# Reordering maxima waves, value products and statistics in the pixel attention of a fused four-block kernel

## The reference, cut to what matters

```
xn  = group_norm(x2, gn_scale, gn_bias)              # 32 groups of 8 channels
q, k, v = split(w_qkv @ xn + b_qkv)                  # 8 heads of 32 channels
w   = softmax(q^T k / sqrt(32), over the 1024 keys)  # 1024 x 1024 per image and head
h   = w @ v
out = x2 + w_proj @ h + b_proj
```

## Time and profile before

| what | value |
|---|---|
| median of the runs | 1919.95 us |
| profiled execution, span | 1922.28, 1920.5 us |
| TensorE busy | 1666.5 us, 87% |
| VectorE busy | 1376.5 us, 72% |
| ScalarE busy | 790.9 us, 41% |
| GpSimd busy | 1360.7 us, 71% |
| chain that ended last | PE 57%, DVE 30%, issue 5%, ACT 3%, POOL 2%, DMA 2% |
| its largest lines | DVE MX L1327 18%, PE AV L684 8%, PE RB L932 6% |
| TensorE waits for L1327 before the weight load of L632 into S | 84.4 us, 195 times |
| one reduction of 128 x 512 to maxima | 681 ns |
| load of an input tile pair (1024 KB), issue to landing | 4.9 us; in the windows shown issued at 859.96 |

### The profile page before, as it was taken

How to read it: one execution, slowest core, us unless ns; L and a number is a source line. 1 busy time by engine, 2 the same in 40 slices (tenths; PEclk the granted TensorE clock), 3 DMA queues, 4 the chain that set the end, 5 groups by cost and what they waited for, 6 DMA issues and landing times.

```text
span 1920.5 us, 37066 instructions
## 1 busy us (share of the span) xinstructions
PE 1666.5 (87%) x15160; PEld 768.6 (40%) x15160; DVE 1376.5 (72%) x2121; ACT 790.9 (41%) x1546; POOL 1360.7 (71%) x581
## 2 busy tenths in 40 slices
PE   6898656799999999999999999999997689889974
PEld 2333223344344444444444444444442355555541
DVE  5767577887777777777777777777771157878875
ACT  0443410255445455454454455454555233333320
POOL 0584500298888878878878878788689068988996
PEclk8898877799999999999999999999998889999986
DMA  5000030300001001010010010010010201222211
GB/s 189 1 2 1 1 129 0 146 15 24 2 23 45 2 24 45 2 46 23 1 60 9 2 67 2 1 67 2 2 46 1 89 29 52 84 82 75 74 51 47
DMA packets 48431, 75.10 MB, mean 39 GB/s; under 512 B 30804, under 2 KB 31110, under 8 KB 48262
## 3 DMA queue, kind: packets, MB, share of 16 engines
q1 hardware_dynamic: 38758, 72.15, 10.5%
q10 hardware_dynamic: 9504, 0.59, 0.3%
HBM read 44.87 MB, written 25.17 MB: 36 GB/s over the span
## 4 chain that ended last, share of the span: by engine, by line
PE 57%; DVE 30%; issue 5%; ACT 3%; POOL 2%; DMA 2%; SPq 0%; POOLq 0%; DVEq 0%; ACTq 0%
DVE MX L1327 18%; PE AV L684 8%; PE RB L932 6%; PE AV L945 3%; PE S L632 3%; PE S L720 3%; PE RB L720 3%; PE RB L981 3%; DVE HI L1304 2%; DVE LO L1305 2%; PE RB L710 2%; PE RB L738 2%; PE RB L745 1%; PE S L606 1%; PE S L960 1%
## 5 line engine op out<-in xcount | busy, mean ns | idle before, releaser
L1238 POOL TENSOR_TENSOR ACC<-ACC,PR 128x1024 f32<-128x1024 f32 x360 | 843.7, 2386 | 25.6 <-ACT PR L1075 25.3
L1075 ACT ACTIVATE PR<-S 128x512 f32<-128x512 f32 x687 | 388.7, 603 | 383.8 <-PE S L670 258.2
L1327 DVE TENSOR_REDUCE MX<-S 128x1 f32<-128x512 f32 x660 | 431.5, 681 | 103.7 <-PE S L632 56.0
L1238 POOL TENSOR_TENSOR ACC<-PR 128x1024 f32<-128x1024 f32 x72 | 169.6, 2379 | 351.7 <-PE S L699 156.3
L684 PE MATMUL AV<-PR,VT 128*32 128x512 f32 x2304 | 306.1, 609 | 2.3 <-ACT PR L1075 2.3
L632 PE MATMUL S<-HI 32*128 32x512 f32 x660 | 259.6, 483 | 17.5 <-DVE MX L1327 11.3
L1075 ACT ACTIVATE PR<-RB 128x512 f32<-128x512 f32 x316 | 187.8, 603 | 101.8 <-PE S L670 42.0
L1327 DVE TENSOR_REDUCE MX<-RB 128x1 f32<-128x512 f32 x300 | 201.3, 680 | 22.3 <-PE RB L632 13.9
L655 PE MATMUL S<-HI 32*128 32x512 f32 x687 | 194.7, 467 | 2.8 <-DVE X L1520 2.3
L632 PEld LDWEIGHTS S<-HI 32*128 32x128 f32 x660 | 106.1, 188 | 189.5 <-DVE MX L1327 84.4
L1264 POOL TENSOR_TENSOR PR<-WO,WRK 128x1792 f32<-128x1792 f32 x32 | 155.4, 4877 | 29.6 <-DMA WO<-WO 17.4
(11 more groups left out here) (352 smaller groups left out, 3477.4 us busy)
## 6 DMA issues: line engine op xcount, KB each, us to landing
X<-out_y SPq DMA_DIRECT2D x24, 1024.0 KB, 4.9
out_y<-X SPq DMA_DIRECT2D x16, 1024.0 KB, 4.7
X<-in_x SPq DMA_DIRECT2D x8, 1024.0 KB, 8.5
OHU<-out_y SPq DMA_DIRECT2D x8, 512.0 KB, 4.0
X<-out_y SPq DMA_DIRECT2D x8, 512.0 KB, 4.0
out_y<-X SPq DMA_DIRECT2D x8, 512.0 KB, 3.1
out_y<-OHU SPq DMA_DIRECT2D x8, 512.0 KB, 3.2
WO<-WO SPq DMA_DIRECT2D x128, 16.0 KB, 1.8
```

The source lines that it names most:

```text
L1075: nc.scalar.activation(exps(s, pair)[:, HALF * one:HALF * one + HALF], RING[ring.place()], ACT.Exp, scale=1.0 if i is None else float(D) * ...
L1238: nc.gpsimd.tensor_tensor(ACC[:, pair, :], so_far, exps(s, pair), ALU.add).then_inc(pool_used, 1)
L1327: nc.vector.tensor_reduce(out=MX[:, h, t, keys:keys + 1], in_=bank(), op=ALU.max, axis=AX.X).then_inc(ring_free, 1)
```

## The change

`values` becomes a job of the list. A half's first step has now both waves in front of its other jobs. A middle step is as before. A half's last step has the max wave, the values of the step before, the late wave, `negate`, its other jobs, its own values, and `flip`. The statistics of a second window (`ahead` = 2) go from steps 11 and 13 to 9 and 12, and the first `gn` from 15 to 13. The ring is filled in the new order. Computation and data stay the same.

```diff
--- before.py
+++ after.py
@@ -110,7 +110,7 @@
 
     if job[0] == "v":
         return 2 if single else 1
-    return {"max": 2, "late": 2, "stats": 0, "negate": 0, "reread": 0, "concepts": 4, "softmax": 0, "turn": 4,
+    return {"max": 2, "late": 2, "stats": 0, "negate": 0, "values": 0, "reread": 0, "concepts": 4, "softmax": 0, "turn": 4,
             "classes": 2, "norms": 2, "pool": 0, "regate": 0, "write": 4}.get(job[0], 1)
 
 
@@ -135,16 +135,8 @@
 
 
     jobs = [[] for _ in range(STEPS)]
-    late = [[] for _ in range(STEPS)]
     for half in range(2):
         first = MT * half
-        if half == 0 or nxt:
-            waves = maxima(1 - half)
-            for step in range(first, first + MT):
-                jobs[step].append(waves.pop(0))
-                late[step] = [("late",) + waves.pop(0)[1:]]
-            jobs[step] += late[step] + [("negate", 1 - half)]
-            late[step] = [("flip", 1 - half)]
         if half == 1 or trail:
             jobs[first + SUM_AT].append(("sums",))
             jobs[first + SPREAD_AT].append(("spread", half - 1))
@@ -157,15 +149,28 @@
         for step, job in zip((3, 5, MT + 4, MT + 7), ((0, 0), (1, 0), (0, 1), (1, 1))):
             jobs[step].append(("post",) + job)
     if ahead:
-        first = MT + 3 if ahead == 2 else MT
+        first = MT + 1 if ahead == 2 else MT
         jobs[first].append(("stats", 0, ahead))
-        jobs[first + (2 if ahead == 2 else 1)].append(("stats", 1, ahead))
+        jobs[first + (3 if ahead == 2 else 1)].append(("stats", 1, ahead))
         jobs[first + (4 if ahead == 2 else 3)].append(("gn", 0, ahead))
     if gn:
         jobs[MT + 5].append(("gn", 1, 1))
     for step, stage in side:
         jobs[step].append(stage)
-    return [job + waves for job, waves in zip(jobs, late)]
+    for half in range(2):
+        waves = maxima(1 - half) if half == 0 or nxt else []
+        for at in range(MT):
+            first, second, rest = waves[:1], [("late",) + wave[1:] for wave in waves[1:2]], jobs[MT * half + at]
+            waves = waves[2:]
+            ends = [("negate", 1 - half)] if first else [], [("flip", 1 - half)] if first else []
+            if at == 0:
+                rest = first + second + rest
+            elif at < MT - 1:
+                rest = first + rest + [("values", 0)] + second
+            else:
+                rest = first + [("values", 0)] + second + ends[0] + rest + [("values", 1)] + ends[1]
+            jobs[MT * half + at] = rest
+    return jobs
 
 
 
@@ -748,15 +753,9 @@
                 for s in range(STEPS):
                     ring.begin(jobs[s], i is None)
                     scores(u, par, s)
-                    last = s % MT == MT - 1
-                    behind = [job for job in jobs[s] if job[0] == ("flip" if last else "late")]
-                    for job in jobs[s][:len(jobs[s]) - len(behind)] + [("values",)] + behind:
+                    for job in jobs[s]:
                         if job[0] == "values":
-
-                            if s % MT:
-                                values(u, par, s - 1)
-                            if last:
-                                values(u, par, s)
+                            values(u, par, s - 1 + job[1])
                         elif job[0] == "spread":
                             spread(2 * u + job[1])
                         elif job[0] == "sums":
@@ -1404,6 +1403,8 @@
                             normalise(1 - par if job[1] else par, 1 if job[1] else 0)
                         elif job[0] == "sums":
                             ring.skip(1)
+                        elif job[0] == "values":
+                            pass
                         elif job[0] == "max" or job[0] == "late":
                             row_max(*job[1:])
                         elif job[0] == "negate":
```

## The result

The changed kernel takes 1934.81 us, the median of five runs (1929.35 to 1939.72), beside 1919.95 (1919.33 to 1923.85) for the kernel before: ratio 1.0077, 95% interval 1.0052 to 1.0102. The forecast was 1920.4 in 1911 to 1930. The profiled execution took 1939.45 (span 1937.7), 17.2 more than that of before, where the medians differ by 14.9.

What follows compares the result with a forecast made beforehand. Neither TensorE nor VectorE alone was the bound; whichever is late sets each step. Terms +6.1 - 1.8 + 0.6 - 1.0 - 1.6 - 0.9 - 0.9 = +0.5 gave 1920.4 us, range 1911 to 1930.

Steps and rivals of the forecast that it cites:

- (a): Last steps of a half, values between the waves: +0.32 in 19 steps (+6.1); with a residual -0.25 each (-1.8).
- (b): First steps with V, both waves in front: 3.50 grows to 4.46, step with sums falls from 5.00 to 4.08; +0.6.
- (c): Second windows, statistics and group sums earlier: steps 12 and 13 +0.91, step 14 -1.37, step 15 +0.23; -1.6 over seven.
- R1: Rival, slower: the step with sums doesn't return the stall in front of V; half of it about 10, 1930; chance 0.12.
- R3: Rival, faster: last steps follow TensorE, 4.6 instead of 5.13, 26 times: -13, 1907; chance 0.08.
- R4: Rival, faster: the moved statistics cost nothing, taken up by VectorE's slack: -11, 1909; chance 0.08.
- R2: Rival, slower: granted clock, one 1.2 GHz stretch in each of 7 windows, +10 less 3: 1927; chance 0.06.
- (d): Once each: batch 0's first window waits 0.9 less for statistics; a values step moved in the layer ahead gives -0.9.

Runs made afterwards that it cites:

- e9: Changed kernel plus one idle VectorE memset of 1024 columns ahead of L2's windows: 1930.84 us, ratio 1.0068 to the kernel before.
- e10: Changed kernel plus one idle VectorE memset of 2048 columns ahead of L2's windows: 1933.33 us, ratio 1.0069 to the kernel before.
- e7: Changed kernel without VectorE's second part of the statistics in second windows, that computation left out: 1912.24 us, ratio 0.9969 to the kernel before.
- e11: Against e8: the changed kernel's orders of waves, values and V everywhere, statistics still in pieces: 1913.54 us, ratio 0.9966 to the kernel before.
- e5: Changed kernel with the old order in the two windows of the layer ahead (L0): 1929.29 us, ratio 1.0047 to the kernel before.
- e8: Kernel before, values between waves only in last steps with a residual, second windows' statistics moved, second part in three pieces: 1899.08 us, ratio 0.9896.
- e4: Changed kernel with the statistics back in steps 11 and 13 and group sums in 15: 1938.95 us, ratio 1.0099 to the kernel before.
- e1: Kernel before with only the second windows' statistics moved to steps 9 and 12, first group sums to 13: 1916.45 us, ratio 0.9989.
- e2: Kernel before with only the values of the step before put between the two waves of last steps: 1933.59 us, ratio 1.0075.
- e3: Kernel before with only both waves put in front of V in a half's first steps that have V: 1923.49 us, ratio 1.0020.
- e6: e4 plus an unused matmul before the flip's wait in L2's windows behind batch 0's first: 1938.71 us, ratio 1.0101 to the kernel before.

## Why the prediction was wrong

**The sum of the steps was right.** (a), (b) and (c) came out within 0.05 per step, as the table shows, but for the 0.08 in step 10: VectorE's hole ahead of the late wave, ScalarE's 0.44 in front of V, the stall returned by the step with sums at 4.07 (R1's condition, over 4.28, was not met), and the statistics' wait turning up in step 13 as late drains. R3 and R4 fall by the same rows: last steps took 5.11 and not 4.6, step 13 took 4.88.

**The step that failed is R2, left out of the sum and held for 0.06.** The prediction put the clock into a rival and its argument against it was "five windows with nearly the same waits hold 1.00". That took undisturbed windows as proof that such waits are harmless. The traces show that a wait can be followed by a slow stretch or not with all steps the same (batches 2 and 5 beside 1, 3, 4 and 6 of the changed kernel; e9, e10), and that the changed kernel has other waits: in an undisturbed second window 1.5 in step 13 and 0.4 to 0.5 before the transposes and before V, where the one of before has 1.0 in step 12 and 1.1 in step 14; in a first window 0.4 to 0.5 before the transpose and before V, where before had none over 0.3. That the kernel before had one stretch in the thirteen windows from batch 1 on said little about the next order. The prediction's own sign of being wrong, a granted clock under 1.00 in windows that had none, is what came: 0.98 and 0.95 in batch 3.

**Its price was too low as well.** R2 counted one stretch per second window at 1.4, from the one window of before that had one; 1927 in all. After, one of 3.4 costs 1.6 (step 0, 6.08 instead of 4.44) and one of 6.8 costs 2.3 to 2.5 (steps 13 and 14, 11.39 instead of 8.92). Five stretches more, and four of the six twice as long as the one of before, are 11.4 of the +12.1 between the starts of batch 1 and of the last window.

**Term (d) failed by the clock too.** The -0.9 of the layer ahead became +3.1; in e7, e9 and e11, whose stretches lie otherwise there, it is -0.7 to -1.0, as forecast. Batch 0's first window, by the prediction's terms some 0.2 shorter (-0.9 for the statistics, twice +0.32), grew by 1.8: its steps 0 and 1 by 2.0, since its first V ran at 1.2 GHz (a stretch from 368.9 to 375.8), the others together by -0.2. The kernel before has a stretch there as well, of 3.4; e5, with V in the new place and a stretch of 3.4, takes 0.5 more than it for these two steps, so some 1.5 of the 2.0 come with the longer stretch.

The Trainium skill ("TensorE: Matmul & The Clock Gate", Part 1: A second HAM failure mode: psum-queue depth-cycling) tells of a bf16 kernel in which TensorE idles briefly again and again between groups of matmuls that cycle through PSUM, often enough for its clock to oscillate between the two levels. The traces here agree: the longest wait right before the stretch at 921.9 is 1.53, on a PSUM bank that VectorE still reads. That case spoke for R2 and was not weighed.

**What stays open.** What decides whether a given wait is followed by a stretch is not settled, beyond that the same wait in the same step is followed by one in one batch and not in the next, and that their places differ between executions with the same steps (e9, e10). In the steps before a stretch single waits of 0.4 to 1.8 stand (one of 3.6 before that of e8), and waits of 0.4 to 1.6 stand in windows without one as well. Each kernel has one trace, so the counts in the table at the end are those of one execution. That fewer and shorter waits make stretches rarer fits this table, but not e4, which lost the wait of 1.5 and has no fewer; it is argued, not shown.

## What to carry to other kernels

Where TensorE is busy nine tenths of the time at full clock, an order that lengthens a wait by 0.3 and returns it in the next step need not be neutral: price slow stretches behind such waits (here 0.9 to 2.5 us each), above all when the trace of before already holds one. Look at busy TensorE time for the same number of matmuls before looking at steps: the 12.4 more pointed to the clock at once. And take the mean granted clock of every run, not only that of the profiled one: e5's trace was its fastest execution. VectorE work without a deadline, put where VectorE waits for a product (pieces of 0.7) or under the sums (1.5 in one piece, 0.08 dearer in the step behind), cost next to nothing, while 1.5 in one piece among the maxima held up TensorE: 7 x 2.56 in the second windows (67.86 to 65.30) are 17.9 of e8's 20. Place and size were changed together, so which of them did it isn't separated.

## What the runs showed of the hardware that was not expected

- A wait of TensorE of 1.5, and also two of 0.4 in close order, in a stream that is over 90% busy, can be followed by 3.4 or 6.8 us at 1.2 GHz; matmuls of values went from 1.07 to 1.93 for eight, V from 2.05 to 3.68 for sixteen.
- Slow stretches that begin between 400 and 1440 of the profiled execution, their count and total length, beside its time (one execution each; that of e5 was the fastest of ten):

| kernel | count, us | profiled time | median |
|---|---|---|---|
| before | 2, 6.8 | 1922.28 | 1919.95 |
| changed | 8, 41.0 | 1939.45 | 1934.81 |
| e1 | 4, 13.7 | 1914.71 | 1916.45 |
| e2 | 7, 23.9 | 1934.68 | 1933.59 |
| e3 | 4, 13.7 | 1924.71 | 1923.49 |
| e4 | 9, 30.7 | 1938.77 | 1938.95 |
| e5 | 4, 13.7 | 1921.05 | 1929.29 |
| e6 | 9, 30.7 | 1942.58 | 1938.71 |
| e7 | 3, 10.2 | 1909.92 | 1912.24 |
| e8 | 1, 3.4 | 1898.94 | 1899.08 |
| e9 | 8, 37.5 | 1930.40 | 1930.84 |
| e10 | 6, 20.5 | 1932.44 | 1933.33 |
| e11 | 4, 13.7 | 1913.68 | 1913.54 |

- The stretches can lock to the loop: in e2, e4 and e6 one in each batch from batch 1 or 3 on, 143.4 apart, at the same offset in the batch within 0.3. In e5 and e10 they come in every second batch, 283.3 apart.
- The same code of L0's second window took 242.1 or 238.1 to 238.4 by where its stretches fell. The spread of the whole goes with it: 1929 to 1940 for the changed kernel, 1898 to 1902 for e8, whose only stretch between 400 and 1440 is at 1431.
